# A graph kernel on one core: the ramp that VectorE compares with moves from SBUF to a bank of PSUM

## The reference

```python
xh = x @ en_weight.T
rel_term = jnp.dot(re_weight @ re_specific_attention, u2)
e = jax.nn.leaky_relu(xh[heads] @ u1 + xh[tails] @ u3 + rel_term)
alpha = jax.nn.softmax(e)                      # one softmax over all 100,000 edges
out = jax.ops.segment_sum(alpha[:, None] * x[tails], heads, num_segments=N_ENT)
```

## Time and profile before

| what | value |
|---|---|
| device time, median of 3 runs | 10093.97 us (10083.33 to 10097.08) |
| span of the profiled execution, first to last instruction | 9138.1 us |
| busy in the span | POOL 72%, DVE 63%, PE 54%, PEld 40%, ACT 9% |
| gathers of this stage (L1846) | 806, from 4447.8 to 5587.4 us |
| scores of this stage (L798) | 806, from 4472.2 to 5585.3 us |

### The profile page before, as it was taken

How to read it: one execution, slowest core, us unless ns; L and a number is a source line. 1 busy time by engine, 2 the same in 40 slices (tenths; PEclk the granted TensorE clock), 3 DMA queues, 4 the chain that set the end, 5 groups by cost and what they waited for, 6 DMA issues and landing times. The chain is left out here.

```text
span 9138.1 us, 79567 instructions
## 1 busy us (share of the span) xinstructions
PE 4929.6 (54%) x17328; PEld 3653.7 (40%) x17328; DVE 5774.6 (63%) x18939; ACT 852.5 (9%) x2178; POOL 6584.3 (72%) x6544
## 2 busy tenths in 40 slices
PE   0466015555555565555666665788884444454444
PEld 0355014344433343334433333555553444443333
DVE  8677028888566656666688887777776444454444
ACT  0000000000000000000233333222221000010000
POOL 5777777777677767777677774766664777747776
PEclk9765557777777777777767766555555555565555
DMA  2344011111211121111211122222221222222222
GB/s 46 70 100 109 1 18 52 52 52 52 60 53 53 53 60 53 53 53 52 58 48 48 48 49 47 52 50 50 50 49 57 53 53 53 53 65 53 53 53 62
DMA packets 397463, 489.89 MB, mean 54 GB/s; under 512 B 135634, under 2 KB 302358, under 8 KB 396726
## 3 DMA queue, kind: packets, MB, share of 16 engines
q0 software_dynamic: 208736, 381.82, 17.5%
q1 hardware_dynamic: 185226, 101.57, 3.9%
q10 hardware_dynamic: 3020, 1.36, 0.1%
HBM read 448.73 MB, written 37.86 MB: 53 GB/s over the span
## 5 line engine op out<-in xcount | busy, mean ns | idle before, releaser
L1832 POOL DMA_INDIRECT RING<-TAB,IDX x2418 | 2319.9, 959 | 807.6 <-issue 683.9
L1295 PE MATMUL PS<-RB,RING 128*128 128x256 f32 x4836 | 1743.7, 524 | 1325.4 <-DMA RING<-TAB,IDX 1285.6
L1295 PEld LDWEIGHTS PS<-RB,RING 128*128 128x128 f32 x4836 | 1217.9, 264 | 1851.0 <-issue 1191.2
L670 DVE TENSOR_TENSOR RA<-RA,PS 128x256 f32 x2418 | 995.2, 412 | 874.9 <-PE PS L1295 833.3
L670 DVE TENSOR_TENSOR RB<-RB,PS 128x128 f32 x2490 | 712.6, 286 | 1194.6 <-PE PS L1295 1173.3
L1295 PE MATMUL PS<-OH,RING 128*128 128x128 f32 x3324 | 809.2, 422 | 912.6 <-DMA RING<-TABM,IDX 409.5
L1781 POOL DMA_INDIRECT REC<-RC x800 | 962.5, 1203 | 299.4 <-issue 243.2
L656 DVE TENSOR_SCALAR RB<-IOTA,KEY,WE 128x256 f32<-128x256 f32 x2418 | 1080.1, 447 | 107.0 <-ACT RA L1618 48.2
L1295 PEld LDWEIGHTS PS<-OH,RING 128*128 128x128 f32 x3324 | 706.0, 314 | 1014.4 <-issue 820.1
L1846 POOL DMA_INDIRECT RING<-TABQ,IDX x806 | 895.1, 1111 | 277.6 <-issue 242.7
L1832 POOL DMA_INDIRECT RING<-TABN,IDX x830 | 787.0, 948 | 365.1 <-issue 252.8
(11 more groups left out here) (377 smaller groups left out, 6684.1 us busy)
## 6 DMA issues: line engine op xcount, KB each, us to landing
RING<-in_edge_attr_dram SPq DMA_DIRECT2D x830, 64.0 KB
RING<-TAB,IDX POOLq DMA_INDIRECT x2418, 2.5
RING<-TABN,IDX POOLq DMA_INDIRECT x830, 2.5
RING<-TABM,IDX POOLq DMA_INDIRECT x830, 2.5
RING<-TABQ,IDX POOLq DMA_INDIRECT x806, 2.6
REC<-RC POOLq DMA_INDIRECT x800, 2.6
TAB<-HN SPq DMA_DIRECT2D x18, 512.0 KB, 3.2
RING<-TABG,IDX POOLq DMA_INDIRECT x560, 2.6
```

Of the source, the lines that this page charges most:

```text
L670: v.tensor_tensor(sl, sl, sums_of(k, weighted), ALU.add).then_inc(s_ad, 1)
L1295: m = t_.matmul(sums_of(t, wide), GD[:, slot_, :], one_hot(t, wide), start=True, stop=True)
L1832: p.indirect_dma_start(GD[:, t % SLOTS, :], None, table, bass.IndirectOffsetOnAxis(ap=idx[:, t:t + 1], axis=0)).then_inc(s_ring[t // 4 % 1 ...
```

## The change

Bank 7 of PSUM is freed: the small products of the running maximum that lay in banks 6 and 7, each in two halves by turns, now all lie in bank 6, the row at columns 0 to 127 and the spread maximum at column 256. TensorE therefore waits, before it writes the row of group g, for the running maximum of group g - 1, not g - 2. Into bank 7 VectorE copies the ramp once. The scores (L798) and the one-hots by fours (L856) then read the ramp there, in float32; the other operand stays in SBUF.

```diff
+        IOTAP = PS[7][:, 0:WN]
...
             v.memset(ZG, 0.0).then_inc(misc.sem, misc.one("zg"))
+            v.tensor_copy(IOTAP, IOTA[:, :]).then_inc(misc.sem, misc.one("iota"))
             v.tensor_scalar(WE0[:, 0:NT0], KEY0[:, 0:NT0], 255.5, -BIG, ALU.is_gt, ALU.mult).then_inc(misc.sem, misc.one())
...
-                    v.tensor_copy(RHS1[:, 128:144], PS[7][:, 0:16]).then_inc(misc.sem, misc.one())
+                    v.tensor_copy(RHS1[:, 128:144], PS[6][:, 0:16]).then_inc(misc.sem, misc.one())
...
-                v.scalar_tensor_tensor(out=junk[:, t % 2, :], in0=IOTA[:, :], scalar=KEY0[:, t:t + 1],
+                v.scalar_tensor_tensor(out=junk[:, t % 2, :], in0=IOTAP, scalar=KEY0[:, t:t + 1],
                                        in1=PB[:, bass.ds(w * WN, WN)], op0=ALU.is_equal, op1=ALU.mult,
                                        accum_out=S0[:, t:t + 1]).then_inc(s_score, 1)
...
                 elif k == 6:
                     v.wait_ge(s_gmax_t, g + 1)
-                    v.tensor_reduce(MR[:, g % 4:g % 4 + 1], PS[6][0:1, g % 2 * 128:g % 2 * 128 + 128], AX_X,
+                    v.tensor_reduce(MR[:, g % 4:g % 4 + 1], PS[6][0:1, 0:128], AX_X,
                                     ALU.max).then_inc(s_gm2, 1)
...
-                        v.tensor_tensor(MG[:, g:g + 1], MG[:, g - 1:g], PS[7][:, g % 2:g % 2 + 1], ALU.max).then_inc(s_gm3, 1)
+                        v.tensor_tensor(MG[:, g:g + 1], MG[:, g - 1:g], PS[6][:, 256:257], ALU.max).then_inc(s_gm3, 1)
...
-                    v.tensor_tensor((OHB, OHT)[a // 4 % 2][:, 0:b - a, :], IOTAB[:, :].unsqueeze(1).to_broadcast([128, b - a, WN]),
+                    v.tensor_tensor((OHB, OHT)[a // 4 % 2][:, 0:b - a, :], IOTAP.unsqueeze(1).to_broadcast([128, b - a, WN]),
                                     KEY0[:, a:b].unsqueeze(2).to_broadcast([128, b - a, WN]), ALU.is_equal).then_inc(s_ohb, 1)
...
                         t_.wait_ge(s_gmax, g + 1)
-                        if g >= 2:
-                            t_.wait_ge(s_gm3, g - 1)
-                        t_.matmul(PS[6][0:1, g % 2 * 128:g % 2 * 128 + 128], GM[:, g:g + 1], IDENT[:, :], start=True,
+                        if g:
+                            t_.wait_ge(s_gm3, g)
+                        t_.matmul(PS[6][0:1, 0:128], GM[:, g:g + 1], IDENT[:, :], start=True,
                                   stop=True).then_inc(s_gmax_t, 1)
                     else:
                         t_.wait_ge(s_gm2, g + 1)
-                        t_.matmul(PS[7][:, g % 2:g % 2 + 1], ONES[0:1, :], MR[:, g % 4:g % 4 + 1], start=True,
+                        t_.matmul(PS[6][:, 256:257], ONES[0:1, :], MR[:, g % 4:g % 4 + 1], start=True,
                                   stop=True).then_inc(s_gm2_t, 1)
```

More of the change, by code:

```diff
@@ L834, in group_step @@
                         v.wait_ge(s_gm3, g)
-                        v.tensor_tensor(MG[:, g:g + 1], MG[:, g - 1:g], PS[7][:, g % 2:g % 2 + 1], ALU.max).then_inc(s_gm3, 1)
+                        v.tensor_tensor(MG[:, g:g + 1], MG[:, g - 1:g], PS[6][:, 256:257], ALU.max).then_inc(s_gm3, 1)
                     else:
-                        v.tensor_copy(MG[:, 0:1], PS[7][:, 0:1]).then_inc(s_gm3, 1)
+                        v.tensor_copy(MG[:, 0:1], PS[6][:, 256:257]).then_inc(s_gm3, 1)
                 else:
@@ L1366, in _ @@
             t_.wait_ge(misc.sem, misc.at["gret"])
-            t_.matmul(PS[7][:, 0:16], RET, ADC[:, :], start=True, stop=True).then_inc(s_misc_t, 1)
+            t_.matmul(PS[6][:, 0:16], RET, ADC[:, :], start=True, stop=True).then_inc(s_misc_t, 1)
             for t in range(NT0 + LAG0 + LATE0 + GS):
```

## The result

The changed kernel takes 10110.19 us (median of 15 runs, 10091.80 to 10121.70), the kernel before on the same chip 10093.08 us (15 runs, 10083.33 to 10105.50). The ratio is 1.0016, with a 95% interval from 1.0009 to 1.0023: a sixth of a per cent slower where 1% less was forecast.

A forecast was written before the change was run, and what follows sets the result against it. POOL's queue was taken as the bound at 1.416 us a tile, VectorE close behind. 100.9 us from VectorE's pace plus 5.98 for the last rows, against 2.4 + 0.4, gave -104: 9990 us, range 9968 to 10060 (81 in 100).

The forecast's parts named there:

- the same 104 us: Whole saving forecast for the softmax-by-source stage, taken from the profile's span and set against the 10093.97 us median.
- POOL: Gathers in this stage fall from 1115 ns to about 950, so POOL's own pace becomes 1.251 us a tile, 0.165 less.
- VectorE as the next bound: With POOL at 1.251 us a tile, VectorE's own work sets the stage's pace, slower by 2%.
- the term of 1.275 us a tile: VectorE's pace in this stage without waits for rows, taken between 1.260 and 1.289 us a tile.
- Reads from PSUM: Ramp reads in VectorE's long instructions: 0 ns more a score, 12 ns more a one-hot by fours, 2.4 us over 202.
- Rival B: Scores and one-hots cost 20 to 80 ns more with the ramp in PSUM: 10010 to 10070 us; 9%.
- the estimate by the Trainium skill's page "Perfetto Trace Analysis": VectorE's scores and one-hots each cost 65 ns more from PSUM: 1.356 us a tile, saving some 40 us, 10054.
- D: Slower: VectorE gets the ramp from PSUM at half the rate, 1.81 us a tile, +290 us, 10384; 3%.
- Bank 6 and the copy: TensorE's added wait for the running maximum costs 0; VectorE's one ramp copy before the stage costs 0.4 us.
- Rival C: POOL's gathers stay held up because the second operand's SBUF path is what is shared: 10094 us, same; 12%.
- A: The forecast case: POOL freed, VectorE the bound at 1.26 to 1.29 us a tile, 9971 to 10010 us; 74%.
- the unseen: Remainder of the chances, something unforeseen anywhere, of either sign: 2%, half counted as faster and half as slower.

The follow-up runs named there:

- c_after: The changed kernel as it is, profiled on a chip where the kernel before took 10092.01 us: 10111.42 us, ratio 1.0015.
- e_bank_only: The changed kernel with both ramp reads back in SBUF, bank sharing and copy kept: 9127.81 us against 9128.49 for the kernel before, ratio 1.000.
- c_before_2: The kernel before, unchanged, profiled on the chip where the changed kernel was also profiled: 10092.01 us.
- c_before: The kernel before, unchanged, profiled again on a chip where its median was 9128.49 us: the profiled run took 9130.74 us, span 9129.0.

## Why the prediction was wrong, step by step

- **"The profile gives no time of its own for the profiled execution ... What the device time holds above the span, 955.9 us by the median, lies before the first and behind the last recorded instruction", and "I set the same 104 us against the median of 10093.97."** This is the step that failed. Each page with its run's time at hand shows 1.7 to 1.8 us outside the span, so the 955.9 us were a difference between chips, spread over the stages with gathers. The bound of that span, POOL's queue at 1.416 us a tile, was carried over to chips where it isn't the bound: there the stage went at 1.489 us a tile before and 1.499 after, held up by late signals, and the 104 us forecast became 17 us more.
- **POOL.** On kind A right: the gather fell to 945 ns for 948 to 955 forecast. On kind B the gather fell as well (1100 to 946 by the mean), but the rate of 1.251 us a tile does not exist there. 805 steps of c_after took 1206.7 us, 1.499 a tile: of POOL's idle time ahead of the gathers, the waits ended by a remote signal grew by 102.6 us and those for TensorE by 36.8.
- **VectorE as the next bound.** Right on kind A, and the term of 1.275 us a tile was 0.027 too high: first to last score took 5475.2 - 4470.2 = 1005.0 us, 1.248 a tile, for 1013 forecast. The rest of VectorE's waits did not grow, as feared, but shrank, while the wait for rows went (the 39.6 us for TensorE in rows 7, over 990 us, became 29.3 over 900). That makes 111.7 us for 104.
- **Reads from PSUM.** No price: a score takes 477 ns on the page (477 before), and 1219 ns is the median of L858 and of L856 alike. Rival B (20 to 80 ns more) is out, and with it the estimate by the Trainium skill's page "Perfetto Trace Analysis", section "Optimizing Scalar/DVE Operations": its 65 ns are not in these durations, nor in the time. The rule of the Trainium skill's page "SBUF — State Buffer", section "Who interferes with whom", held on both kinds: one reader moved at a time took 43 and 120 ns off the gather on kind A, both together 168 (154 on kind B). D is out by the same rows.
- **Bank 6 and the copy.** Right: e_bank_only at 1.000.
- **Rival C** gives the time that came (10094, the same), but not its mechanism: it had the gather held up as before, and the gather was freed. That its number fits is luck. The small loss on kind B (0 to 20 us) has no explanation here; the added idle time of POOL (130.1 us) just exceeds what went (124.2 us).
- **The chances.** A, B and half of the unseen add up to 84 in 100, not 83; nothing hangs on it. No rival was a state of the chip in which another bound holds.

Shown: the two kinds of chip, the saving on one, its return as waiting on the other, that semaphores rise there microseconds behind the work that raises them, by their recorded times (5.5 and 11.3 us in the two cases followed), and that with fewer gather instructions the waiting goes. Not shown: where a signal spends that time. Not known: why the chips differ, what in a gather instruction brings it about, and whether the recording has a part in it.

## What to carry to other kernels

Before a saving is worked out, hold the profiled execution's span against the times it is to be set against; a difference of 10% that no row explains is a sign that another bound may hold where the time is measured, not an offset. When an engine's instructions get shorter and its idle time grows by as much, read what ends the idle time in both traces, and where it is "remote", hold the time at which the semaphore rose against the end of the instruction that raises it. Taking one operand of VectorE's long instructions out of SBUF does free POOL's gathers, at no price for VectorE in these rows, and it pays where POOL's own pace is the bound.

## What was not expected of the hardware

- Chips that run this same program in 9127 and in 10024 to 10094 us, with equal durations of single instructions (gathers 947 and 948 ns, scores 478 and 478 by the mean in c_before_2 and c_before) and nearly equal clock (0.644 and 0.656 over the run).
- All engines standing still together, 3.62 us in the timeline above, behind a signal recorded 11.3 us after the work; and VectorE waiting 5.54 us for a signal that it had raised itself.
- 32 rows a gather in place of 128 bring POOL's time for it only from 944 to 872 ns, while a plain load of 128 rows takes it 534 ns.
